# The triangular solve in two steps: the second quarter's own product and its coupling term added in PSUM, with the inverse times the raw coupling block made ahead

## The reference

```python
def step(S, inps):
    qi, ki, vi, bi = inps
    pred = jnp.einsum('bhkv,bhk->bhv', S, ki)
    S = S + bi[..., None, None] * ki[..., :, None] * (vi - pred)[..., None, :]
    o = jnp.einsum('bhkv,bhk->bhv', S, qi)
    return (S, o)
S0 = jnp.zeros((b, H, DK, DV), x.dtype)
_, o = jax.lax.scan(step, S0, (qt, kt, vt, bt))
```

## Time and profile before

| what | us |
|---|---|
| median of 3 runs | 306.08 |
| lowest and highest run | 305.58, 307.73 |
| profiled execution | 305.82 |
| its span from the first to the last instruction | 304.0 |
| PE busy in the span | 270.7 |
| DVE busy in the span | 205.3 |
| ACT busy in the span | 92.8 |

### The profile page before, as it was taken

The page is one execution under the profiler, slowest core; times in us unless marked ns, Lnnn a source line. Parts: engine busy times, 40 slices in busy tenths (PEclk is TensorE's granted clock), DMA queues, the critical chain, the costliest instruction groups (busy, mean ns, idle before and its releaser), DMA issues.

```text
span 304.0 us, 9882 instructions
## 1 busy us (share of the span) xinstructions
PE 270.7 (89%) x4469; PEld 208.8 (69%) x4469; DVE 205.3 (68%) x408; ACT 92.8 (31%) x230; POOL 32.6 (11%) x29
## 2 busy tenths in 40 slices
PE   8899999999888998978989997976889999679865
PEld 8466677779687986858777765755877676455442
DVE  3559869987848566467678488563766264497992
ACT  1023301320000026656225434473414243141210
POOL 1981100210293000000000000000000000000000
PEclk9999999999999999989978999997995999869999
DMA  7999800000000000000002105100000000000001
GB/s 296 423 418 421 381 3 0 0 0 0 2 0 2 0 1 3 2 4 0 2 4 74 68 1 213 80 4 2 1 4 2 2 0 0 0 1 2 0 0 43
DMA packets 2730, 18.71 MB, mean 62 GB/s; under 512 B 464, under 2 KB 784, under 8 KB 1936
## 3 DMA queue, kind: packets, MB, share of 16 engines
q1 hardware_dynamic: 2704, 18.34, 15.2%
HBM read 18.01 MB, written 0.33 MB: 60 GB/s over the span
## 4 chain that ended last, share of the span: by engine, by line
PE 65%; DVE 27%; issue 4%; ACT 2%; DMA 1%; DVEq 0%; ACTq 0%
PE ps L1217 13%; PE ps L1530 8%; PE ps L1261 4%; PE ps L1626 3%; PE ps L1511 3%; PE ps L1635 3%; PE ps L1275 3%; PE ps L1737 2%; DVE big L1061 2%; PE ps L1686 2%; PE ps L1374 2%; DVE wt L1058 2%; PE ps L1779 2%; PE ps L1703 2%; PE ps L1657 2%
## 5 line engine op out<-in xcount | busy, mean ns | idle before, releaser
L1217 PE MATMUL ps<-big,cwb 128*128 128x384 f32 x120 | 40.8, 490 | 1.2 <-DVE cwb L684 1.0
L1217 PEld LDWEIGHTS ps<-big,cwb 128*128 128x128 f32 x120 | 22.3, 190 | 15.4 <-DVE cwb L684 1.6
L1530 PE MATMUL ps<-xT,wl 128*128 128x320 f32 x88 | 24.5, 434 | 0.7 <-ACT wguT L355 0.5
L288 POOL TENSOR_TENSOR xs<-xs,big 128x640 f32<-128x640 f32 x14 | 22.3, 1595 | 3.9 <-DVE sc L761 2.6
L1626 PE MATMUL ps<-wt,big 32*32 32x32 f32 x1280 | 14.9, 201 | 8.0 <-issue 3.0
L1530 PEld LDWEIGHTS ps<-xT,wl 128*128 128x128 f32 x88 | 16.6, 190 | 7.8 <-ACT wguT L355 0.7
L1626 PEld LDWEIGHTS ps<-wt,big 32*32 32x32 f32 x1280 | 13.3, 112 | 10.1 <-DVE wt L1015 3.9
L331 ACT COPY pecT<-ps 128x384 f32<-128x384 f32 x12 | 5.7, 478 | 41.7 <-PE ps L1217 41.7
L1058 DVE COPY_PREDICATED wt<-cst,ps 128x320 f32<-128x320 int32 x16 | 8.0, 499 | 14.5 <-PE ps L1635 14.5
L1275 PE MATMUL ps<-wt,pecT 128*128 128x256 f32 x72 | 16.6, 381 | 0.8 <-DVE big L783 0.8
L1261 PE MATMUL ps<-wt,pecT 128*128 128x256 f32 x72 | 17.0, 381 | 0.0
(11 more groups left out here) (292 smaller groups left out, 526.6 us busy)
## 6 DMA issues: line engine op xcount, KB each, us to landing
big<-in_patches SPq DMA_DIRECT2D x6, 960.0 KB, 11.8
wl<-in_layers SPq DMA_DIRECT2D x2, 2176.0 KB, 19.9
wf<-in_ffn SPq DMA_DIRECT2D x1, 2112.0 KB, 17.8
wl<-in_layers SPq DMA_DIRECT2D x2, 1040.0 KB, 15.9
wt<-in_tok SPq DMA_DIRECT2D x1, 1536.0 KB, 24.7
wt<-in_tok SPq DMA_DIRECT2D x1, 768.0 KB, 8.4
cwb<-in_conv SPq DMA_DIRECT2D x1, 640.0 KB, 3.9
cst<-in_constants SPq DMA_DIRECT2D x1, 320.0 KB, 25.0
```

The lines of the kernel that those rows point to most:

```text
L288: nc.gpsimd.tensor_tensor(xs[:, hf], old, new, ALU.add).then_inc(S["xsum"], 1)
L1217: last = mm(ps[:, i % 4, 0:GRP], cwc[:, k, c * P:(c + 1) * P], xg[:, g, k, :], start=(k == 0), stop=(k == KC - 1))
L1530: last = mm(ps[:, bank, 0:NT], w(c, j), x[:, c, :], start=(c == 0), stop=(c == CH - 1))
```

## The change

The second quarter's solution is T (b + A u1), with T its inverse and A the coupling block (sign and scale included). Before, b + A u1 was formed first and then multiplied by T. Now T times A is made first, from the unscaled key products (the scale comes as a factor of each row, by DVE from PSUM), and T b and (T A) u1 are added in PSUM.

- ACT makes a copy of the unscaled key products of the second quarters (`gram`), in two pieces: 4 column blocks (groups) right behind line 487, the other 16 behind its copy of the third loop pass. `gram` and `cross` lie in the buffer `xs`, which is free by then.
- PE: for each half b `second_into_first` (40 pairs, banks 6 and 7) and `own_quarter` for all four quarters (80 pairs, banks 4 and 5, the second quarters left open for accumulation); then for each half `first_into_second` (40 pairs) adds the coupling term. The query-norm products go from ahead of the solve to two places behind it, one ahead of the outputs and one between their row halves.
- DVE: one multiply of 128x320 for each half in place of two additions of 32x320 to `bv`.

```diff
+        xf = xs[:, :, :, :].rearrange("p a k n -> p (a k n)")
+        gram = xf[:, 0:640].rearrange("p (g n) -> p g n", g=NG)
+        cross = xf[:, 640:1280].rearrange("p (g n) -> p g n", g=NG)
@@ ACT, layer @@
                 nc.scalar.copy(apm[:, 16:NG, :], ps[:, 4:8, 0:P]).then_inc(S["p5"], 1)
+                nc.scalar.copy(gram[:, 16:NG, :], ps[:, 4:8, 0:32]).then_inc(S["p5"], 1)
...
                 y_out(3, 0)
                 y_out(3, 1)
+                act_.wait_ge(S["pm"], EACH["pm"] * (l + 1))
+                nc.scalar.copy(gram[:, 0:16, :].rearrange("p (j h) n -> p h j n", h=HP),
+                               ps[:, 0:4, :].rearrange("p h (j n) -> p h j n", n=P)[:, :, :, 0:32]).then_inc(S["gram"], 1)
@@ DVE, layer @@
                 for b in range(2):
+                    dve.wait_ge(S["cross_mm"], EACH["cross_mm"] * l + b + 1)
+                    v.tensor_tensor(cross[:, NB * b:NB * (b + 1), :], bank32(6 + b, slice(0, P)),
+                                    negc[:, NB * b:NB * (b + 1)].unsqueeze(2).broadcast_to([P, NB, 32]), ALU.mult
+                                    ).then_inc(S["cross"], 1)
                     dve.wait_ge(S["u1_mm"], EACH["u1_mm"] * l + b + 1)
-                    v.tensor_copy(half(uc, 2, b), ps[64:96, 4 + b, 0:NT]).then_inc(S["u1_two"], 1)
-
-                for b in range(2):
-                    dve.wait_ge(S["r_mm"], EACH["r_mm"] * l + b + 1)
-                    for a in range(2):
-                        q = 2 * a + 1
-                        v.tensor_tensor(half(bv, q, b), half(bv, q, b), ps[32 * q:32 * q + 32, 6 + b, 0:NT], ALU.add
-                                        ).then_inc(S["b2"], 1)
+                    v.tensor_copy(half(uc, 2, b), ps[64:96, 4 + b, 0:NT]).then_inc(S["cross"], 1)
@@ PE, layer @@
-                pe.wait_ge(S["p5"], EACH["p5"] * l + 1)
+                pe.wait_ge(S["p5"], EACH["p5"] * l + 2)
...
-                pe.wait_ge(S["pm"], EACH["pm"] * (l + 1))
-                pe.wait_ge(S["silu"], EACH["silu"] * (l + 1))
-                for j in range(CH):
-                    mm(ps[:, 2 + j, 0:NT], blk, kqsq[:, 1, j, :], start=True, stop=False)
-
-                def solve(rows, b):
+                def second_into_first(b):
 
                     for g in range(NB * b, NB * (b + 1)):
-                        for q in rows:
+                        for a in range(2):
+                            late = slice(64 * a + 32, 64 * a + 64)
+                            last = mm(ps[64 * a:64 * a + 32, 6 + b, 32 * (g % NB):32 * (g % NB) + 32], gram[late, g, :],
+                                      ttc[late, g, :], start=True, stop=True)
+                    last.then_inc(S["cross_mm"], 1)
+
+                def own_quarter(b):
+
+                    for g in range(NB * b, NB * (b + 1)):
+                        for q in range(4):
                             r = slice(32 * q, 32 * q + 32)
                             last = mm(ps[r, 4 + b, 32 * (g % NB):32 * (g % NB) + 32], ttc[r, g, :],
-                                      bv[r, g, :], start=True, stop=True)
-                    return last
...
+                                      bv[r, g, :], start=(q % 2 == 0 or g == NB * b), stop=(q % 2 == 0))
+                    last.then_inc(S["u1_mm"], 1)
+
+                def first_into_second(b):
+
+                    pe.wait_ge(S["cross"], EACH["cross"] * l + 2 * b + 2)
+                    pe.wait_ge(S["u1"], EACH["u1"] * l + b + 1)
+                    for g in range(NB * b, NB * (b + 1)):
+                        for a in range(2):
+                            early = slice(64 * a, 64 * a + 32)
+                            last = mm(ps[64 * a + 32:64 * a + 64, 4 + b, 32 * (g % NB):32 * (g % NB) + 32],
+                                      cross[early, g, :], uc[early, g, :], start=False, stop=(g == NB * b + NB - 1))
+                    last.then_inc(S["u2_mm"], 1)
+
+                def query_norm(j):
+
+                    mm(ps[:, 2 + j, 0:NT], blk, kqsq[:, 1, j, :], start=True, stop=False)
+
+                pe.wait_ge(S["gram"], l + 1)
                 pe.wait_ge(S["bv"], EACH["bv"] * (l + 1))
                 for b in range(2):
                     pe.wait_ge(S["t"], b + 1)
-                    solve((0, 2), b).then_inc(S["u1_mm"], 1)
+                    second_into_first(b)
+                    own_quarter(b)
                 pe.sem_inc(S["t"], -2)
                 for b in range(2):
...
-                for b in range(2):
-                    pe.wait_ge(S["b2"], EACH["b2"] * l + 2 * b + 2)
-                    solve((1, 3), b).then_inc(S["u2_mm"], 1)
+                    first_into_second(b)
+                pe.wait_ge(S["pm"], EACH["pm"] * (l + 1))
+                pe.wait_ge(S["silu"], EACH["silu"] * (l + 1))
+                query_norm(0)
...
                 last.then_inc(S["o_first"], 1)
+                query_norm(1)
                 pe.wait_ge(S["u2_two"], EACH["u2_two"] * l + 2)
```

More of the change, by code:

```diff
@@ L217, in build @@
         EACH = {
-            "lwa": 16, "lwb": 16, "x": 4, "n_sq": 2, "n_ms": 2, "n_rs": 4, "h": 2, "wgs": 2, "gs": FC, "ys": FC, "kq_mm": 2, "p5": 1, "pm": 2, "b_mm": 1,
+            "lwa": 16, "lwb": 16, "x": 4, "n_sq": 2, "n_ms": 2, "n_rs": 4, "h": 2, "wgs": 2, "gs": FC, "ys": FC, "kq_mm": 2, "p5": 2, "pm": 2, "b_mm": 1,
             "v_mm": 2, "silu": 7, "ss_mm": 1, "ss": 1, "c": 1, "bm": 3, "sr": 2, "bv": 1, "ap_mm": 2, "ap": 3, "y_mm": 2 * (LEVELS - 1), "pairs": 4, "y": 2 * (LEVELS - 1),
-            "z_mm": 2 * (LEVELS - 1), "tp": 2 * (LEVELS - 1), "t": 0, "u1_mm": 2, "u1": 2, "u1_two": 2, "r_mm": 2, "b2": 4, "u2_mm": 2, "u2": 2, "u2_two": 2,
+            "z_mm": 2 * (LEVELS - 1), "tp": 2 * (LEVELS - 1), "t": 0, "gram": 1, "cross_mm": 2, "cross": 4, "u1_mm": 2, "u1": 2, "u2_mm": 2, "u2": 2, "u2_two": 2,
             "o_first": 1, "o_mm": 2, "osq": 2, "oss_mm": 2, "ors": 4, "oT": 2, "wo_mm": 2, "up_mm": FC, "sg": FC,
@@ L1688, in outputs @@
                     return last
-                pe.wait_ge(S["b2"], EACH["b2"] * (l + 1))
-                pe.wait_ge(S["pm"], EACH["pm"] * (l + 1))
                 for b in range(2):
```

## The result

The changed kernel takes 313.18 us (median of 5 runs, 312.27 to 316.85), the kernel before 306.33 (5 runs, 305.58 to 308.28): a ratio of 1.0232 with an interval of 1.0168 to 1.0297. It is slower by about 7 us, where 4.3 were forecast.

The account below looks back on a forecast made before the run. PE and its waits, including instruction-block fetches, were taken as the bound. Layer 0 +3.3, loop -1.4 and layer 1 +2.4 summed to +4.3 us: profiled 305.82 gives 310.1, plus 0.26 for the median, 310.4 us; range 304.5 to 314.3.

Parts of the forecast that it names:

- the block bounds: Limits of 3.4 and 4.3 us per instruction block on PE, said to move the sum by -1.6 to +2.
- rival (c): Layer 1's first loop pass: the taken branch drops the order for the next block; 313.3 us, chance 0.22.
- The block, 3.8 us: PE fetches its program in blocks of 128 pairs, one block ahead, each taking 3.8 us.
- The clock credits, -0.6 and -0.8: Taken off layers 0 and 1 behind the solves' outputs, since products there would meet full clock sooner.
- the prices behind the second pause: Layer 0's solve: 58 pairs 1.5 us, query norms 1.1 each, outputs 1.0; layer 1: 20 pairs 0.5, the rest alike.
- The loop, -1.4: Layer 1's loop: the pause at the branch moves 79 pairs ahead, gaining 1.4 us (between 0.5 and 2).
- (a): Rival: blocks arrive in time because idle PE's sequencer can order ahead; -4.6, 301.5 us, chance 0.07.
- (b): Rival: as forecast, but the clock stays full through the solve; 308.5 us, chance 0.2.
- (d): Rival: blocks take 3.0 us instead of 3.8, half-hidden; 307.2 us, or 305.3 with full clock; chance 0.1.
- The costs taken at nothing: ACT's two copies of raw products, the new waits, DVE's queued quarter-2 copy and PSUM accumulation were given no cost.

Follow-up runs that it names:

- blocks_alone: PE alone, computing nothing of the reference: 512 small products in straight code took 27.7 us; the same kind in a loop took 2.5 us per pass of 256 pairs.
- norms_only: The kernel before with only the query-norm products moved to the change's two later places: 309.93 us, ratio 1.0130.
- norms_in_pause: The changed kernel with both query-norm products put between the two halves' first products: 308.76 us.
- four_fewer: The kernel before with three clock-keeping products ahead of layer 1's loop replaced by two of 480 columns: 304.15 us, ratio 0.9926.
- pauses_filled: norms_in_pause with two more wide products, results unused, ahead of each layer's coupling products: 308.52 us over ten executions.
- merged: The change with second-quarter own and coupling products made one (240 pairs), norms between the halves, and four_fewer's two wide products: 302.57 us, ratio 0.9841 against the kernel before.

## Why the prediction was right, and where it was mis-sized

**Right: the mechanism and its places.** That code arrives in blocks of 128 pairs, that 80 more pairs move the borders forward by 80, and where the pauses end followed from counting, and all five pauses in the first loop pass of layer 1 and in the solves came there, within two pairs. blocks_alone shows the cadence without the rest of the kernel. The direction was right, and the measured 313.18 lies in the range, in its upper part. That it lies inside owes something to luck: the block bounds alone give 310.4 - 1.6 = 308.8 to 312.4, and the stated ends 304.5 and 314.3 follow from no sum that is shown. The number is even that of rival (c), 313.3, whose mechanism did not happen.

**The block, 3.8 us.** In layer 0 resumes came 3.5 apart (153.62, 157.08), in layer 1 3.8 (231.62, 235.40), alone 3.73. The term was good to 0.3 us.

**The clock credits, -0.6 and -0.8, and the prices behind the second pause were mis-sized.** I took the credits because the output norm and what follows it would come when PE had worked longer without a pause. But the clock is at half for 5.5 and 6.7 us behind O, as it was (5.3 and 6.8), so nothing is given back. The products behind the second pause started at half clock and PE stayed there for 13.6 us in both layers, where it had been 6.8 and 10.2. The query norms, taken at 1.1 us each, cost 1.36 by their starts, and row half 0 of the outputs 1.22 instead of 1.0. From the second resume to O were forecast 4.7 us in layer 0 and 3.7 in layer 1; it took 5.6 and 4.6. Without the credits as well, that is 3.2 us over both layers, less 0.6 for the shorter blocks of layer 0 and some tenths in layer 1.

**What the sum didn't say: that the norms' place is the price.** The prediction had them in its sum (two of 1.1 us behind the pauses) but named the 80 pairs as the cause. norms_only and norms_in_pause turn this round: by the medians the move costs 3.5 to 4.4 us and the 80 pairs 1.9 to 2.5. The work was free where PE waits for the inverse and for its next block, and in the old order it lay just there.

**The loop, -1.4, came to -0.5.** The 2.97 at the branch went, as counted. From the second half of the first products to the next pass it is 5.40 us where it was 6.15 (209.43 - 203.28): -0.75. But the half clock at the new pause lasts from 212.6 to 219.4, 6.8 us instead of 3.4, and takes a part back: up to T of layer 1 the gain is 0.46. four_fewer shows what the border is worth when nothing else takes its place, 2.2.

**The rivals.** (a), blocks in time, fell: pauses of 1.4 to 2.4 us at the five borders, and 3.73 us per block with nothing else running. The rule "mostly hidden" of the Trainium skill (Runtime: NRT & Kernel Launch, section Instruction fetch mechanics) therefore doesn't hold for rows of 32x32 products. (b), full clock through the solve, fell by the rows at 0.50; and in layer 0 of pauses_filled what the full clock gained was lost again at the next border. (c), the branch drops the order, didn't happen: no pause stands at the first products of layer 1's solve. Whether the order was saved only because the transfer began just ahead of the branch is open. (d) fell with (a). The costs taken at nothing on ACT and DVE stayed nothing.

**What stays open.** The medians differ by 6.9 us, the two solves by 8.1 in the profiles. The loop gives back 0.2 to 0.5. The rest, some 0.7 to 1 us, may be the difference between executions, whose own spread (312.27 to 316.85) goes with a granted clock between 0.938 and 0.919. What decides how long PE stays at half after such a pause was not settled, nor whether a full clock through both solves would gain anything (pauses_filled).

## What to carry to other kernels

Count instructions as well as arithmetic: where PE runs small products in straight code, each 128 matmuls with their weight loads cost about 3.7 us in these runs (3.4 to 4.3), though PE was through with them in some 2 us (1.93 in blocks_alone, 2.1 in layer 0's solve). So a form with fewer products can beat one with less waiting between them: merged takes 302.57 us and norms_in_pause, with 80 pairs more, 308.76, of which the loop's border is worth some 2.2. Products that depend on nothing are worth most where PE stands still anyway, ahead of a pause or inside it; moved behind the last pause they are paid in full, and at half clock. And a border that falls on a loop's branch can be moved away by a few instructions ahead of it.

## What the runs showed that I had not expected

- Moving two products of 1.3 us in all to places 7 and 9 us later costs 3.5 (norms_only).
- 1024 pairs cost 27.7 us in straight code, at half clock, and 1792 in a loop 17.4, at full (blocks_alone). By their own pace at half clock (1.93 us per 128) the 1024 would have taken 15.4. The first pass of that loop (256 pairs, 2.35 us) had no pause at all: the block ahead had come during the wide products.
- Four instructions fewer ahead of a loop gave 2.2 us (four_fewer).
- Two more wide products in a pause kept the clock at full for 10.4 us, and whether that gained up to 2 us or nothing can't be told (pauses_filled).
